# Loads of the sheared band issued by ScalarE, stores of T alone in SyncE's queue, four slots in DRAM

## The chip, the core and the metric

The kernel runs on one core of a Trainium2 chip. The metric is the device time of one execution in microseconds (us). The engines are named as in the profile: PE is TensorE (PEld its weight loads), DVE is VectorE, ACT is ScalarE, POOL is GpSimd, and SP is SyncE, which in this kernel does nothing but issue transfers. ACTq or SPq is an engine's instruction sequencer, which waits, branches and issues transfers while the engine's arithmetic may go on.

## What is computed

A layer norm feeds two branches, an attention with relative positions and a mixture of experts (top 2 of 8), and both are added to x. The change touches the attention alone, and there the term that adds q times the relative key:

```python
# x: (2, 2048, 256), 16 heads of 16, MAX_LEN 256; 2 batches x 16 heads = 32 heads below
rel_pos = jnp.arange(L)[None, :] - jnp.arange(L)[:, None] + (MAX_LEN - 1)
rel_k = relative_k[rel_pos]                       # out of range: wraps once, then clips
rel_v = relative_v[rel_pos]
scores = jnp.einsum('bhld,bhrd->bhlr', Q, K) * scale
scores = scores + jnp.einsum('bhld,lrd->bhlr', Q, rel_k)
attn = jax.nn.softmax(scores, axis=-1)
out = jnp.einsum('bhlr,bhrd->bhld', attn, V) + jnp.einsum('bhlr,lrd->bhld', attn, rel_v)
```

## The kernel before

The program has three stages: `project` (norm, q, k, v; up to about 180 us), `attend` (about 180 to 3440 us), and `mix` (output projection and experts). Only `attend` is changed.

`attend` works on 512 units. A unit is 128 query rows of one head, so a head has 16 units, and 2 heads (`STEP` = 32 units) make one turn of a loop in the program; `pipeline` writes the first 23 steps and the last ones out and loops over the rest. One step k does different parts of several units: the relative product T of unit k, the scores and their maximum of unit k-3, the row with the maximum of unit k-4 (`q_max`), the transposed scores and exponentials of unit k-5, the values of unit k-6, and the relative values of earlier half heads.

The path of T, with which the change deals, is this. PE multiplies the unit's queries by the relative keys (L875), 128 x 768. ACT copies the product from PSUM to `rel[k % 2]` (`rel_evac`, L1039, two copies of 128 x 384). SP stores it to `rel_scratch` in DRAM, a slot of 128 rows of 1280 words (L772, one or two transfers), and reads it back with a row pitch that is one word shorter (L762, `skew_src`), so that row p comes back shifted by p: the sheared band, up to 128 x 1152, in `skewed[u % 4]`. DVE adds the band to the scores when it looks for the maximum (`search_bank`, L1116 near the diagonal, L1120 elsewhere), and PE adds it in the transposed scores (L923).

Each engine runs its instructions in the order in which the program writes them. In step k, SP's are: wait until T of unit k-1 is stored (`s_gw`, L755) and until the band's buffer is free (`s_x`, L759), load the band of unit k-1 (L762), wait for ACT's copies of unit k (`s_ge`, L766) and for the load of unit k-2, which reads the same of the two slots (L769), store T of unit k (L772). In steps 5 to 10 of a head (`LOAD0` = 5) follow one q and one k transfer each for the next head (`load_stacks`, L703 and L706, both on one semaphore `s_stk`), in step 5 also the v rows (L712).

ACT's order in step k is: exponentials 0 and 1 of unit k-5 (L1047), the low half of the maximum (L1061), the two copies of T of unit k (L1039), exponentials 2 and 3, the copy of `q_max` of unit k-4 (L1071), and two or more casts of exponentials (L1055). The copy of T of unit k waits at L1037 until T of unit k-2 is stored, as there are two `rel` buffers. PE begins a step with the first two turned score tiles, which need `q_max`, and DVE searches the scores with the band. POOL makes the low parts of the exponentials (L839) and, in steps 7 to 10 of a head, the parts of the next head's v (L824 to L828).

Of the kernel before, what the change touches and what calls it, by code (L numbers as in the profile page):

```python
# [563 lines left out]
def attend(nc, hbm, keep):  # L564

    with ExitStack() as ctx:
# [36 lines left out]

        s_stk = [sem(f"b_stacks{i}") for i in range(2)]
        s_vi = [sem(f"b_v_in{i}") for i in range(2)]
# [89 lines left out]

        def load_stacks(sp, it, head, planes=range(6)):

            b = head % 2
            for j in planes:
                s, tile = j % 3, j // 3  # L700
                rows = bass.ds((it + head // 2) * DK, DK)
                r0 = tile * ROW_TILE + DK * s
                sp.dma_start(q_stack[b][r0:r0 + DK, :],  # L703
                             hbm["planes"][0, Q_PLANES[s], rows, b * L:(b + 1) * L]).then_inc(s_stk[b], 16)
                keys = hbm["planes"][1:1 + KINDS, K_PLANES[s], rows, b * L + tile * HALF_L:b * L + (tile + 1) * HALF_L]
                sp.dma_start(k_stack[b][r0:r0 + DK, :, :], keys.rearrange("v d n -> d v n")).then_inc(s_stk[b], 16)  # L706

# [5 lines left out]

        STK = 12 * 16

# [27 lines left out]
        def _(sp):  # L743
# [3 lines left out]
            sp.nop(nofuse=True)  # L747
            load_stacks(sp, 0, 0)
            load_v(sp, 0, 0)

            def step(it, k):
                u = k - 1
                if exists(it, u):

                    sp.wait_ge(s_gw[u % 2], stored(it, u))  # L755
                    sp.nop(nofuse=True)
                    if u >= 4:
                        for s in s_x:
                            sp.wait_ge(s, it * (2 * STEP) + 2 * (u - 3))  # L759
                            sp.nop(nofuse=True)  # L760
                    w = blocks(u % NB) * P
                    sp.dma_start(skewed[u % 4][:, 0:w], skew_src(u % 2, w)).then_inc(s_gr[u % 4], 16)  # L762
                u = k
                if exists(it, u):

                    sp.wait_ge(s_ge, it * (2 * STEP) + 2 * u + 2)  # L766
                    sp.nop(nofuse=True)
                    if u >= 2:
                        sp.wait_ge(s_gr[(u - 2) % 4], uses(it, u - 2, 4, 16))  # L769
                        sp.nop(nofuse=True)  # L770
                    for to, a, w in rel_pieces(u % NB):
                        sp.dma_start(hbm["rel_scratch"][u % 2, :, to:to + w], rel[u % 2][:, a:a + w]).then_inc(s_gw[u % 2], 16)  # L772
                if LOAD0 <= k % NB < LOAD0 + 6 and exists(it, (k // NB + 1) * NB):

                    head = k // NB + 1
                    if head >= 2 and k % NB == LOAD0:
                        for s in s_x:
                            sp.wait_ge(s, it * (2 * STEP) + 2 * NB * (head - 1))
                            sp.nop(nofuse=True)
                    load_stacks(sp, it, head, [k % NB - LOAD0])  # L780
                    if k % NB == LOAD0:
                        if head >= 2:
                            sp.wait_ge(s_vp, 2 + it * (2 * len(V_STAGES)) + (head - 1) * len(V_STAGES))
                            sp.nop(nofuse=True)
                        load_v(sp, it, head)
# [80 lines left out]
        def _(pe):  # L866
            def rel_products(it, k):

                c = k % NB
                if c == 0:  # L870

                    pe.wait_ge(s_stk[(k // NB) % 2], it * STK + (k // NB // 2 + 1) * STK)
                for tile in range(2):
                    wait_bank(it, "rel", k, tile)
                    nc.tensor.matmul(bank_of("rel", k, tile)[:, 0:RELN // 2],  # L875
                                     q_stack[(k // NB) % 2][tile_rows(tile), c * P:(c + 1) * P],
                                     keep["rk_stack"][tile_rows(tile), :], start=True, stop=True).then_inc(s_g, 1)

            def score_banks(it, k, pair):

                c, b = k % NB, (k // NB) % 2
                banks = (pair, pair + 2)
                lists = [[seg for seg in segments(c) if seg[0] == bank] for bank in banks]
                for bank in sorted(banks, key=lambda n: len(lists[banks.index(n)])):
# [146 lines left out]
        def _(act):  # L1031
# [17 lines left out]
            def high_part(it, u, e):  # L1049
# [6 lines left out]
                ins.then_inc(s_ha, 1)  # L1056

            def maximum_low(it, u):

# [15 lines left out]
            def step(it, k):  # L1075
# [9 lines left out]
                if turning:  # L1085
                    exponentials(it, k - LAG_X, 2)
                    exponentials(it, k - LAG_X, 3)
                if exists(it, k - LAG_A):
                    query_rows(it, k - LAG_A)
# [695 lines left out]
def program(nc, hbm):  # L1785
    with ExitStack() as ctx:
# [10 lines left out]
        hbm["planes"] = nc.dram_tensor("planes_scratch", (1 + KINDS, 2, D, TOK), FP16, kind="Internal").ap()  # L1797
        hbm["rel_scratch"] = nc.dram_tensor("rel_scratch", (2, P, RELW), FP32, kind="Internal").ap()
        hbm["v_rows"] = nc.dram_tensor("v_rows_scratch", (H, P, NT, DK), FP32, kind="Internal").ap()
# [58 lines left out]
```

## Time and profile before

| | |
|---|---|
| median of 3 runs | 3974.83 us (3958.41 to 4023.03) |
| the profiled execution | 4002.26 us, span 4000.5 us |
| busy share of the span | PE 87%, POOL 69%, ACT 66%, DVE 62% |
| `attend`, 200 to 3400 us | PE 2865, POOL 2561, ACT 2386, DVE 2096 of 3200 us |
| mean granted clock of PE | 0.913 (1.0 is 2.4 GHz, 0.5 is 1.2 GHz) |
| moved | 703 MB, of which queue q1 (all of SP's transfers) 674 MB |

A busy time is the union of an engine's instructions. Weight loads overlap matmuls, so PE's busy time counts stretches in which one is in flight, not work at full rate. Idle time stands with what ended it. A sequencer's waits aren't busy time; SP's are shown in a list of their own.

### The profile page before, as it was taken

The page shows a single profiled execution, that of the slowest core. Times are in us where ns is not written, and L with a number is a line of the kernel's source. Part 1 is how long each engine was busy: PE and PEld are TensorE (multiplying, and loading weights), DVE is VectorE, ACT ScalarE, POOL GpSimd, SP SyncE. Part 2 cuts the span into 40 slices and gives each one's busy share as a digit, 9 for nine tenths or more (in the row PEclk, how much of TensorE's full clock was granted, in tenths as well). Part 3 has the DMA queues.
Part 4 walks back from the last instruction along what each step waited for, and adds up shares of the span by engine and source line. Part 5 has one row for each costly group of instructions (what it writes and reads, how often), then busy time and mean ns, then how long its engine had stood idle before and what let it go on. Part 6 is the DMA issues. An engine that isn't in the chain of part 4 may idle for free. (4 is left out here: it accounts for less than half of the span.)

```text
span 4000.5 us, 177840 instructions
## 1 busy us (share of the span) xinstructions
PE 3468.4 (87%) x65430; PEld 2705.7 (68%) x65430; DVE 2470.0 (62%) x7245; ACT 2646.1 (66%) x5852; POOL 2748.4 (69%) x3015
## 2 busy tenths in 40 slices
PE   7488989898989898989898989899989899799991
PEld 4266767676767676666676767677767677559990
DVE  6366667666667666656675666666667666544443
ACT  3277777777767776767676777777778777224440
POOL 0187878787878787878787888787888788550006
PEclk9689999999989999989898999998999999659995
DMA  8765656565656565656565656565666565542224
GB/s 270 239 200 171 192 176 193 178 186 179 187 174 191 175 193 170 188 170 188 169 194 163 188 179 193 175 193 181 187 184 191 176 186 175 186 166 65 65 62 134
DMA packets 345830, 703.29 MB, mean 176 GB/s; under 512 B 58009, under 2 KB 157186, under 8 KB 343826
## 3 DMA queue, kind: packets, MB, share of 16 engines
q1 hardware_dynamic: 338706, 673.92, 54.5%
q0 software_dynamic: 6144, 16.79, 1.3%
q8 instruction: 556, 9.11, 0.9%
q14 instruction: 424, 3.47, 0.3%
HBM read 343.02 MB, written 347.46 MB: 173 GB/s over the span
## 5 line engine op out<-in xcount | busy, mean ns | idle before, releaser
L839 POOL TENSOR_TENSOR pt_near<-pt_full,pt_near 128x512 f16<-128x512 f32 (+3 forms) x2176 | 2000.8, 948 | 633.1 <-DVE pt_near L1140 565.6
L1047 ACT ACTIVATE pt_full<-pb,exp_bias 128x512 f32<-128x512 f32 x2048 | 1312.6, 693 | 582.0 <-PE pb L931 545.6
L1120 DVE TENSOR_REDUCE part_max<-pb 128x1 f32<-128x512 f32 (+3 forms) x1376 | 771.8, 575 | 513.0 <-DMA skewed<-rel_scratch 317.9
L1116 DVE CUSTOM_DVE_ANT_0 near_sum<-pb,skewed 128x512 bf16<-128x512 f32 (+3 forms) x1216 | 676.2, 572 | 339.3 <-PE pb L889 304.4
L983 PE MATMUL pb<-pt_near,table_high 128*128 128x64 f16 (+6 forms) x18432 | 873.7, 190 | 1.6 <-DVE rel_out L1163 0.8
L983 PE MATMUL pb<-pt_near,table_low 128*128 128x64 f16 (+6 forms) x9216 | 857.7, 191 | 0.0
L983 PEld LDWEIGHTS pb<-pt_near,table_high 128*128 128x128 f16 x18432 | 829.7, 99 | 1.9 <-DVE rel_out L1163 0.9
L983 PEld LDWEIGHTS pb<-pt_near,table_low 128*128 128x128 f16 x9216 | 800.3, 99 | 0.2 <-issue 0.2
L923 PE MATMUL pb<-ident,skewed 128*128 128x128 f32 x3840 | 674.8, 296 | 109.4 <-issue 54.2
L1039 ACT COPY rel<-pb 128x384 f32<-128x384 f32 x1024 | 439.4, 485 | 285.7 <-DMA rel_scratch<-rel 239.3
L957 PEld LDWEIGHTS pb<-v_head,pt_near 128*128 128x128 f16 x13440 | 435.3, 97 | 201.2 <-issue 138.7
L1140 DVE CAST pt_near<-pt_full 128x512 f16<-128x512 f32 (+3 forms) x1280 | 541.4, 473 | 5.4 <-ACT pt_full L1047 5.4
L923 PEld LDWEIGHTS pb<-ident,skewed 128*128 128x128 f32 x3840 | 433.6, 148 | 163.5 <-ACT pt_full L1047 80.8
L957 PE MATMUL pb<-v_head,pt_near 128*128 128x33 f16 x13440 | 518.1, 179 | 15.8 <-POOL pt_near L839 13.5
L889 PE MATMUL pb<-k_stack,q_stack 48*128 48x512 f16 (+3 forms) x2592 | 475.0, 348 | 52.6 <-DVE part_max L1116 28.8
L931 PE MATMUL pb<-q_max,k_stack 50*128 50x128 f16 x8192 | 422.2, 225 | 42.9 <-ACT pt_full L1047 37.2
L839 POOL TENSOR_TENSOR pt_far<-pt_full,pt_far 128x512 f16<-128x512 f32 (+3 forms) x416 | 440.1, 1058 | 0.0
L1055 ACT CAST pt_near<-pt_full 128x512 f16<-128x512 f32 (+3 forms) x896 | 432.6, 539 | 0.0
L931 PEld LDWEIGHTS pb<-q_max,k_stack 50*128 50x128 f16 x8192 | 239.6, 96 | 225.0 <-issue 125.3
L1439 POOL DMA_INDIRECT stage<-y_slots_scratch,slot x64 | 60.7, 949 | 366.0 <-DMA y_slots_scratch<-y_group 346.8
L1055 ACT CAST pt_far<-pt_full 128x512 f16<-128x512 f32 (+3 forms) x416 | 253.1, 608 | 0.0
L889 PEld LDWEIGHTS pb<-k_stack,q_stack 48*128 48x128 f16 x2592 | 149.1, 97 | 121.3 <-DVE part_max L1116 61.3
(182 smaller groups left out, 4046.4 us busy)
## 6 DMA issues: line engine op xcount, KB each, us to landing
skewed<-rel_scratch SPq DMA_DIRECT2D x256, 576.0 KB, 4.8
rel_scratch<-rel SPq DMA_DIRECT2D x416, 319.5 KB, 5.3
rel_scratch<-rel SPq DMA_DIRECT2D x320, 320.0 KB, 4.6
skewed<-rel_scratch SPq DMA_DIRECT2D x64, 512.0 KB, 4.5
skewed<-rel_scratch SPq DMA_DIRECT2D x64, 448.0 KB, 3.9
k_stack<-planes_scratch SPq DMA_DIRECT2D x192, 96.0 KB, 5.1
planes_scratch<-planes SPq DMA_DIRECT2D x64, 256.0 KB, 4.2
rel_scratch<-rel SPq DMA_DIRECT2D x64, 256.0 KB, 4.5
```

The source lines that it names most:

```text
L839: ins = nc.gpsimd.tensor_tensor(pt_piece(c, 1, a, z, near), pt_full[e][:, (a - 4 * g) * P:(z - 4 * g) * P], pt_piece(c, 0, a, z, near), AL ...
L889: ins = nc.tensor.matmul(ps[:, a - bank * CH:z - bank * CH], q_stack[b][tile_rows(tile), c * P:(c + 1) * P], k_stack[b][tile_rows(tile), k ...
L923: nc.tensor.matmul(x_ps[e % 2][:, (blk - 4 * g) * P:(blk - 4 * g + 1) * P], skewed[u % 4][:, col:col + P], keep["ident"][:, :], is_transpo ...
L931: ins = nc.tensor.matmul(x_ps[e % 2][:, i * P:(i + 1) * P], k_stack[b][tile_rows(tile, STACK + 2), kind_of(c, blk), col:col + P], q_max[u ...
L957: ins = nc.tensor.matmul(o_ps[:, i * VW:(i + 1) * VW], src[:, cols], rhs, start=(blk == 0 and part == 0), stop=(blk == NB - 1 and part == 1))
L983: ins = nc.tensor.matmul(acc[:, c0:c1, :], keep[table][:, w:w + P], pt_near[half][:, part, c0:c1, d - M_LO, a * SHIFTS:(a + 1) * SHIFTS], ...
L1039: nc.scalar.copy(rel[k % 2][:, n * half:(n + 1) * half], bank_of("rel", k, n)[:, 0:half]).then_inc(s_ge, 1)
L1047: nc.scalar.activation(pt_full[e][:, :], x_ps[e % 2][:, :], ACT.Exp, bias=exp_bias[:, 0:1]).then_inc(s_exp, 1)
L1055: ins = nc.scalar.copy(pt_piece(c, 0, a, z, near), pt_full[e][:, (a - 4 * g) * P:(z - 4 * g) * P])
L1116: ins = nc.vector.tensor_tensor_reduce(out=near_sum[:, col:col + z - a], in0=src, in1=skewed[k % 4][:, col:col + z - a], scale=1.0, scalar ...
L1120: ins = nc.vector.tensor_reduce(best, src, axis=AX.X, op=ALU.max)
L1140: ins = nc.vector.tensor_copy(pt_piece(c, 0, a, z, near), pt_full[e][:, (a - 4 * g) * P:(z - 4 * g) * P])
```

## The change

ACT now issues the band's load (`load_sheared`), once a step, behind exponentials 2 and 3 and ahead of the `q_max` copy. SP issues the stores of T, with no load between them. `rel_scratch` has four slots instead of two, so the store of unit k waits for the load of unit k-4. The next head's q and k transfers are issued one per step: q in steps 5 to 10 of a head, k in steps 10 to 15, on semaphores of their own; PE waits for the k ones where the first scores of a head are made. The transfers, their number and their sizes are the same.

```diff
-        s_stk = [sem(f"b_stacks{i}") for i in range(2)]
+        s_qin = [sem(f"b_queries{i}") for i in range(2)]
+        s_kin = [sem(f"b_keys{i}") for i in range(2)]
...
             def step(it, k):
-                u = k - 1
+                u = k
                 if exists(it, u):
 
-                    sp.wait_ge(s_gw[u % 2], stored(it, u))
+                    sp.wait_ge(s_ge, it * (2 * STEP) + 2 * u + 2)
                     sp.nop(nofuse=True)
                     if u >= 4:
-                        for s in s_x:
-                            sp.wait_ge(s, it * (2 * STEP) + 2 * (u - 3))
-                            sp.nop(nofuse=True)
-                    w = blocks(u % NB) * P
-                    sp.dma_start(skewed[u % 4][:, 0:w], skew_src(u % 2, w)).then_inc(s_gr[u % 4], 16)
-                u = k
-                if exists(it, u):
-
-                    sp.wait_ge(s_ge, it * (2 * STEP) + 2 * u + 2)
-                    sp.nop(nofuse=True)
-                    if u >= 2:
-                        sp.wait_ge(s_gr[(u - 2) % 4], uses(it, u - 2, 4, 16))
+                        sp.wait_ge(s_gr[u % 4], uses(it, u - 4, 4, 16))
                         sp.nop(nofuse=True)
                     for to, a, w in rel_pieces(u % NB):
-                        sp.dma_start(hbm["rel_scratch"][u % 2, :, to:to + w], rel[u % 2][:, a:a + w]).then_inc(s_gw[u % 2], 16)
-                if LOAD0 <= k % NB < LOAD0 + 6 and exists(it, (k // NB + 1) * NB):
-
-                    head = k // NB + 1
-                    if head >= 2 and k % NB == LOAD0:
+                        sp.dma_start(hbm["rel_scratch"][u % 4, :, to:to + w], rel[u % 2][:, a:a + w]).then_inc(s_gw[u % 2], 16)
+                if LOAD0 <= k % NB and exists(it, (k // NB + 1) * NB):
+
+                    head, j = k // NB + 1, k % NB - LOAD0
+                    if head >= 2 and j == 0:
...
-                    load_stacks(sp, it, head, [k % NB - LOAD0])
-                    if k % NB == LOAD0:
+                    if j < 6:
+                        load_queries(sp, it, head, [j])
+                    if j >= 5:
+                        load_keys(sp, it, head, [j - 5])
+                    if j == 0:
...
+                if c == 0 and pair == 0:
+
+                    pe.wait_ge(s_kin[b], it * STK + (k // NB // 2 + 1) * STK)
...
+            def load_sheared(it, u):
+
+                act.wait_ge(s_gw[u % 2], stored(it, u))
+                if u >= 4:
+
+                    for s in s_x:
+                        act.wait_ge(s, it * (2 * STEP) + 2 * (u - 3))
+                act.nop(nofuse=True)
+                w = blocks(u % NB) * P
+                act.dma_start(skewed[u % 4][:, 0:w], skew_src(u % 4, w)).then_inc(s_gr[u % 4], 16)
+
...
                 if turning:
                     exponentials(it, k - LAG_X, 2)
                     exponentials(it, k - LAG_X, 3)
+                if exists(it, k - 1):
+                    load_sheared(it, k - 1)
                 if exists(it, k - LAG_A):
                     query_rows(it, k - LAG_A)
...
-        hbm["rel_scratch"] = nc.dram_tensor("rel_scratch", (2, P, RELW), FP32, kind="Internal").ap()
+        hbm["rel_scratch"] = nc.dram_tensor("rel_scratch", (4, P, RELW), FP32, kind="Internal").ap()
```

SP's queue before, from the store of unit 13 of a head to the store of unit 15 (steps 13 to 15, ahead of the loop): a load of the band stands in front of each pair of stores, and its wait for `b_rel_stored` is the wait for the stores just above it.

```order
175 L772 DMA rel_scratch<-rel 128x640 [waits b_rel_on_chip,b_skewed3]
176 L772 DMA rel_scratch<-rel 128x639
177 L762 DMA skewed<-rel_scratch 128x1152 [waits b_rel_stored1,b_turned_scores0,b_turned_scores1]
178 L772 DMA rel_scratch<-rel 128x640 [waits b_rel_on_chip,b_skewed0]
179 L772 DMA rel_scratch<-rel 128x512
180 L762 DMA skewed<-rel_scratch 128x1024 [waits b_rel_stored0,b_turned_scores0,b_turned_scores1]
181 L772 DMA rel_scratch<-rel 128x640 [waits b_rel_on_chip,b_skewed1]
```

SP's queue after, steps 14 and 15 of a head (in the loop): stores wait for ACT's copies (`b_rel_on_chip`) and for a load four units back, and one transfer of the next head's k stands between.

```order
215 L765 REGISTER_ALU
216 L771 DMA rel_scratch<-rel 128x640 [waits b_rel_on_chip,b_skewed2]
217 L771 DMA rel_scratch<-rel 128x512
218 L715 DMA k_stack<-planes_scratch 16x3x1024
219 L765 REGISTER_ALU
220 L771 DMA rel_scratch<-rel 128x640 [waits b_rel_on_chip,b_skewed3]
```

SP no longer waits for a store to land. ACT's queue before, from the copies of T to the next step's first exponential:

```order
162 L1039 COPY rel<-pb 128x384 [waits b_rel_stored0,b_rel_product]
163 L1039 COPY rel<-pb 128x384 [waits b_rel_product]
164 L1047 ACTIVATE pt_full<-pb,exp_bias 128x512 [waits b_low,b_turned_scores0]
165 L1047 ACTIVATE pt_full<-pb,exp_bias 128x512 [waits b_low,b_turned_scores1]
166 L1071 CAST q_max<-pb 128x128 [waits b_turned_scores1,b_turned_scores0,b_max_turned]
167 L1055 CAST pt_near<-pt_full 128x512 [waits b_pt_used,b_exp]
```

And ACT's queue after, a step of the same kind:

```order
173 L1044 COPY rel<-pb 128x384 [waits b_rel_stored0,b_rel_product]
174 L1044 COPY rel<-pb 128x384 [waits b_rel_product]
175 L1052 ACTIVATE pt_full<-pb,exp_bias 128x512 [waits b_low,b_turned_scores0]
176 L1052 ACTIVATE pt_full<-pb,exp_bias 128x512 [waits b_low,b_turned_scores1]
177 L1072 DMA skewed<-rel_scratch 128x1152 [waits b_turned_scores1,b_rel_stored1,b_turned_scores0]
178 L1087 CAST q_max<-pb 128x128 [waits b_turned_scores1,b_turned_scores0,b_max_turned]
```

The load has come between the last exponential and the `q_max` copy, with the wait for the stores of the unit before (`b_rel_stored1` beside the copies' `b_rel_stored0`). Its waits for `b_turned_scores` are for the same tiles as the exponentials above it.

## Rows read from the trace of the kernel before

**Rows 1.** Windows: busy us per engine (instructions), PEclk, DMA share, GB/s; `attend`.

```profile
200.00:3400.00 3200.00, 2865.14 (x60899) 2237.03 (x60899) 2096.40 (x6454) 2385.52 (x5369) 2560.68 (x2825) 0.94 0.60 183
```

**Rows 2.** Waits, 200 to 3300 us: us in total, times, longest.

```profile
SPq L756 <- DMA rel_scratch<-rel: 1754.6, 475, 6.8
...
DVE part_max L1120 <- DMA skewed<-rel_scratch: 302.3, 157, 5.1
...
ACT rel L1039 <- DMA rel_scratch<-rel: 228.5, 170, 3.8
...
PE pb L923 <- issue: 54.2, 13, 5.9
```

**Rows 3.** SP's timeline in an even head: start us, duration us, issue.

```profile
2067.68 0.32 SPq L762 DMA_DIRECT2D skewed<-rel_scratch  x1
2068.22 0.80 SPq L772 DMA_DIRECT2D rel_scratch<-rel  x2
2074.15 0.32 SPq L762 DMA_DIRECT2D skewed<-rel_scratch  x1
```

**Rows 4.** SP's timeline in an odd head, and ACT's copy of T there.

```profile
2160.08 0.82 SPq L772 DMA_DIRECT2D rel_scratch<-rel  x2
...
2167.74 0.35 SPq L762 DMA_DIRECT2D skewed<-rel_scratch  x1
...
2167.50 0.86 ACT L1039 COPY rel<-pb 128x384 f32<-128x384 f32 x2 [3.00 <-DMA rel_scratch<-rel]
```

**Rows 5.** ACT's timeline in an even head; in brackets the idle time ahead.

```profile
2009.38 0.86 ACT L1039 COPY rel<-pb 128x384 f32<-128x384 f32 x2
...
2014.77 0.86 ACT L1039 COPY rel<-pb 128x384 f32<-128x384 f32 x2
...
2016.92 0.26 ACT L1071 CAST q_max<-pb 128x128 f16<-128x128 f32 x1
...
2018.81 1.27 ACT L1047 ACTIVATE pt_full<-pb,exp_bias 128x512 f32<-128x512 f32 x2 [0.59 <-PE pb L931]
...
2025.77 1.27 ACT L1047 ACTIVATE pt_full<-pb,exp_bias 128x512 f32<-128x512 f32 x2 [2.40 <-PE pb L931]
...
2030.95 1.27 ACT L1047 ACTIVATE pt_full<-pb,exp_bias 128x512 f32<-128x512 f32 x2 [0.61 <-PE pb L931]
```

**Rows 6.** PE's timeline: the picks of a half head; the start of a loop turn.

```profile
2022.91 1.94 PE L998 MATMUL pb<-pick_dim,rel_out 128*128 128x16 f32 x16
...
2128.37 1.11 PE L923 MATMUL pb<-ident,skewed 128*128 128x128 f32 x4 [4.52 <-issue]
```

**Rows 7.** One instruction per unit, L1071: first and last start.

```profile
L1071 ACT CAST q_max<-pb x512: 257/286/302, 194.4 to 3406.2; 128x128 f16<-128x128 f32 x171
```

**Rows 8.** Transfers: count, KB each, median us from issue to landing.

```profile
skewed<-rel_scratch SPq DMA_DIRECT2D x256, 576.0 KB, 4.8
rel_scratch<-rel SPq DMA_DIRECT2D x416, 319.5 KB, 5.3
...
y_slots_scratch<-y_group SPq DMA_DIRECT2D x39, 256.0 KB, 2.2
```

**Rows 9.** Landing times of the stores at L772; busy tenths of the DMA engines, 2060 to 2096.

```profile
DMA to landing us min/median/max: 2.0/4.7/8.0
...
DMA  4059998105879940489895109599800998910388
```

**Rows 10.** Windows, columns as in rows 1.

```profile
2036.00:2060.00 24.00, 21.78 (x470) 17.43 (x464) 19.04 (x50) 19.04 (x42) 23.43 (x28) 0.93 0.74 235
...
2120.00:2132.00 12.00, 6.93 (x139) 5.02 (x134) 4.75 (x15) 6.01 (x15) 4.55 (x4) 0.84 0.81 235
2132.00:2138.00 6.00, 5.89 (x113) 4.58 (x109) 3.27 (x11) 4.12 (x10) 5.39 (x7) 0.74 0.16 40
...
2156.00:2168.00 12.00, 8.24 (x164) 5.83 (x158) 7.04 (x27) 6.64 (x15) 7.54 (x11) 1.00 0.48 150
2168.00:2180.00 12.00, 10.46 (x199) 9.22 (x199) 5.04 (x17) 7.39 (x16) 7.29 (x10) 0.72 0.60 170
```

More of the change, by code:

```diff
@@ L694, in tile_rows, with load_queries @@
             return slice(tile * ROW_TILE, tile * ROW_TILE + n)
-        def load_stacks(sp, it, head, planes=range(6)):
+        def load_queries(sp, it, head, parts=range(6)):
             b = head % 2
-            for j in planes:
+            for j in parts:
                 s, tile = j % 3, j // 3
@@ L703, in load_stacks, with load_keys @@
                 sp.dma_start(q_stack[b][r0:r0 + DK, :],
-                             hbm["planes"][0, Q_PLANES[s], rows, b * L:(b + 1) * L]).then_inc(s_stk[b], 16)
+                             hbm["planes"][0, Q_PLANES[s], rows, b * L:(b + 1) * L]).then_inc(s_qin[b], 16)
+        def load_keys(sp, it, head, parts=range(6)):
+            b = head % 2
+            for j in parts:
+                s, tile = j % 3, j // 3
+                rows = bass.ds((it + head // 2) * DK, DK)
+                r0 = tile * ROW_TILE + DK * s
                 keys = hbm["planes"][1:1 + KINDS, K_PLANES[s], rows, b * L + tile * HALF_L:b * L + (tile + 1) * HALF_L]
-                sp.dma_start(k_stack[b][r0:r0 + DK, :, :], keys.rearrange("v d n -> d v n")).then_inc(s_stk[b], 16)
+                sp.dma_start(k_stack[b][r0:r0 + DK, :, :], keys.rearrange("v d n -> d v n")).then_inc(s_kin[b], 16)
         def load_v(sp, it, head):
@@ L712, in load_v @@
             sp.dma_start(v_in[b][:, :, :], src.rearrange("o p n d -> p (o n) d")).then_inc(s_vi[b], 16)
-        STK = 12 * 16
+        STK = 6 * 16
         def near_block(half, part, c, d, a, z):
@@ L747, in _ @@
             sp.nop(nofuse=True)
-            load_stacks(sp, 0, 0)
+            load_queries(sp, 0, 0)
+            load_keys(sp, 0, 0)
             load_v(sp, 0, 0)
             def step(it, k):
-                u = k - 1
-                if exists(it, u):
-                    sp.wait_ge(s_gw[u % 2], stored(it, u))
-                    sp.nop(nofuse=True)
-                    if u >= 4:
-                        for s in s_x:
-                            sp.wait_ge(s, it * (2 * STEP) + 2 * (u - 3))
-                            sp.nop(nofuse=True)
-                    w = blocks(u % NB) * P
-                    sp.dma_start(skewed[u % 4][:, 0:w], skew_src(u % 2, w)).then_inc(s_gr[u % 4], 16)
                 u = k
@@ L870, in rel_products @@
                 if c == 0:
-                    pe.wait_ge(s_stk[(k // NB) % 2], it * STK + (k // NB // 2 + 1) * STK)
+                    pe.wait_ge(s_qin[(k // NB) % 2], it * STK + (k // NB // 2 + 1) * STK)
                 for tile in range(2):
@@ L1056, in high_part @@
                 ins.then_inc(s_ha, 1)
+            def load_sheared(it, u):
+                act.wait_ge(s_gw[u % 2], stored(it, u))
+                if u >= 4:
+                    for s in s_x:
[3 more added lines that the diff above has]
+                act.dma_start(skewed[u % 4][:, 0:w], skew_src(u % 4, w)).then_inc(s_gr[u % 4], 16)
             def maximum_low(it, u):
```

## The prediction

> **What bounds the kernel now.** I read the windows first. In `attend`, which is 3,200 of 4,000 us, no engine is full: PE has something in flight 90% of the time, POOL 80%, ACT 75% [rows 1]. So some round of waits must set the pace, and the list of waits says which [rows 2]. SP waited 475 times, 1754.6 us in all, for the store of T to land before it could issue the load of the band. ACT waited 228.5 us in 170 steps for the same stores (its `rel` buffer is free only then), and DVE 302.3 us for the bands that are loaded behind them.
>
> SP's timeline shows the round. In an even head the band's load goes out at 2067.68, the stores of the next T 0.54 us later at 2068.22, and the next load at 2074.15, when those stores have landed [rows 3]. The store waits behind the load in SP's one queue, the next load waits for the store, and a turn takes 6.47 us. In an odd head the stores issued at 2160.08 are waited for until 2167.74, 7.66 us, so a turn takes 8.2 us; ACT sits idle 3.00 us before its copy of T at 2167.50, which is when they landed [rows 4]. Where the round doesn't bind, a step is shorter: ACT's copies of T follow each other at 2009.38 and 2014.77 (5.39 us), and first exponentials at 2025.77 and 2030.95 (5.18 us), and there ACT waits for PE, 0.59 and 0.61 us, not for a transfer [rows 5]. I take 5.3 us as a free step. The average over all units is (3406.2 - 194.4) / 511 = 6.285 us, 100.6 us a head [rows 7].
>
> **Is it the transfers' amount, or their waiting in turn?** Between 2060 and 2096 us the DMA engines' busy tenths run 4 0 5 9 9 9 8 1 0 and again: idle between one turn's landing and the next turn's first packets [rows 9]. That is a chain with gaps, not full engines. A wide unit moves 576 + 640 KB [rows 8], which at 5.3 us a step is 235 GB/s, and 235 GB/s was moved in 2036 to 2060 at a share of 0.74 [rows 10].
>
> **The change, part by part.**
>
> *SP's queue without the loads.* The stores of unit k no longer wait for the store of k-1 to land, nor lie behind a 576 KB load issued 0.54 us earlier. This unties the round above. The time that the store then takes has no row. Below, 256 KB alone land in 2.2 us [rows 8]; above, the longest landing at L772 is 8.0 us [rows 9]. The load still runs at the same time in part, now issued about 1.3 us after the store instead of before it. I take 5.3 us, the median that stands with a load in front [rows 8], as the side on which I would rather err.
>
> *ACT's new wait.* The store of T of unit k-1 must have landed when ACT comes to the load in step k. The time it has: from the end of the copies, 2009.38 + 0.86 = 2010.24, to the end of the next step's last exponential, at 2016.92 where `q_max` starts [rows 5]: 6.7 us. It needs up to 0.8 us for the two issues and 5.3 us to land, 6.1 us: no stall in an ordinary step, 0.6 us to spare. In odd heads it may stall at times. Queued behind the wait on ACT are the `q_max` copy and the casts; PE's turned scores and POOL's low parts wait for those.
>
> *ACT's issue.* On SP one issue lasts 0.32 us, and 0.54 us pass from it to the next [rows 3]. On ACT no row shows one, so the cost per unit lies between 0 (the sequencer issues while the exponentials still run) and 0.54 us. ACT waits 0.6 us a step for PE [rows 5], which covers even the upper end. I take 0. If the cover were gone, 512 x 0.54 = 276 us.
>
> *The band's landing.* DVE needs it about 1.3 steps after its issue or later (it is loaded in step k and searched in step k+2), some 7 us, and it takes 4.8 us [rows 8]. DVE's 302.3 us go, and cost nothing by themselves.
>
> *Four slots, and k a step later.* The wait for the load of unit k-4 is for one issued three steps before: 0. The k transfers end in step 15, and are first needed in step 3 of the next head, four steps later: 0. SP issues one of them behind a store instead of two, and with 0.8 us of stores [rows 3] in a step of 5.3 us it has time for either.
>
> **The sum.** A head after the change, from free steps: 14 steps of 5.3 us and 2 in which PE picks (1.94 us of matmuls at L998 [rows 6]; first exponentials 2018.81 and 2025.77, so 6.96 us [rows 5]) make 88.1 us. POOL is the next bound where it also makes the v parts: it was busy 23.43 of 24 us in 2036 to 2060 [rows 10]. I add 0.7 us in two steps, 1.4 us. What the change doesn't touch: at the start of a loop turn PE stands still, 4.52 us in the one shown [rows 6], 54.2 us in 13 [rows 2], and the clock is low afterwards (0.74 in 2132 to 2138 [rows 10]). About 6.8 us at 1.2 GHz instead of 2.4 lose at most 3.4 us. So (4.2 + 3.4) x 13 / 32 = 3.1 us a head. Together 92.6 us, against 100.6 us now: 8.0 us a head, 256 us in 32 heads.
>
> I check this against the waits. ACT's stalls are 228.5 us; 170 x 0.6 us of that would be spent waiting for PE anyway, which leaves 126 us. The other part is PE's clock. It is 0.94 in `attend` [rows 1], so 12% of 3200 us, 384 us, were at 1.2 GHz, with at most 192 us lost, of which 44 us belong to the loop turns: at most 148 us. They follow gaps in PE's work: in 2156 to 2168 PE was busy 8.24 of 12 us, and in 2168 to 2180 the clock was 0.72; the same after 6.93 of 12 us in 2120 to 2132 [rows 10]. 126 + 148 = 274 us, close to 256.
>
> That is what is gained if every stall and every fall of the clock outside the loop turns goes. Some will stay: late stores in odd heads, POOL's two steps, the picks. I take four fifths, 205 us: 4002 - 205 = 3797 us for the profiled execution. The median shown is 0.9931 of it (3974.83 / 4002.26), so 3771 us; I say 3770.
>
> The Trainium skill's page "DMA: Bandwidth & Descriptors" (section "Issuing engines are not separate DMA queues") says that transfers started by different engines run on the same 16 DMA engines and interleave, and that spreading them only saves the time of issuing. By that rule alone the change would save little. It speaks of bandwidth, and the gaps in the DMA row are at odds with it as a bound here; the first rival below is its case. The page's section on queues adds that each DMA engine takes turns between SP's and ACT's rings; no run before shows it.
>
> **The rivals.**
>
> *Only the issue is saved (chance 0.13).* The load and the store still share the engines and stretch each other, so that a turn is shorter by no more than the 0.54 us from load to store. 170 stalled steps x 0.54 = 92 us, and about half of it is lost again where ACT issues (170 x 0.32 = 54 us). Then 4002 - 38 = 3964, median 3937. For: in 2036 to 2060 the DMA share is already 0.74 [rows 10]. Against: the idle tenths [rows 9].
>
> *ACT pays for the issue in full (0.04).* 4002 + 276 - 205 = 4073, or with the 0.6 us of cover near 3800. The middle, 3936, is a median of 3909. Against it stands ACT's idle time.
>
> *ACT is held at the load: slower (0.06).* The wait stands in an engine that the whole round runs through. From the load's place to the end of the copies of the next step but one ACT needs 2014.77 + 0.86 - 2016.92 + 5.39 = 4.1 us [rows 5]. If a store lands L us after its copies, two steps take L + 4.1 us. That is as slow as the 6.47 us of now from L = 8.8 us on. With the longest landing, 8.0 us [rows 9], and both issues, and some more for the load that runs with it, L = 9.6 and a step is 6.85 us. In the 11 wide units of each head 352 x 0.4 = 140 us are lost: 4142, median 4114. It needs stores that land twice as late as their median, all the time.
>
> *Nothing moves (0.03).* PE or POOL bound it at the present pace, the stalls being covered. The free steps of 5.2 to 5.4 us speak against it.
>
> **The numbers.** The forecast has 0.74, with 3710 to 3860 as its own range. About 2% can be told from no change in this kernel, that is 3895. Faster: the forecast, and the luckier part of the second rival, 0.77. Within 2%: 0.17. Slower: 0.06. Below, all 256 us give 3746 or a median of 3720, and free steps 0.1 us shorter another 45 us less; I set 3690. Above I reach to 3895, which leaves out most of the rivals.
>
> **What would show it.** SP's waits for its own stores are gone and ACT waits at the new load by less than 0.3 us on average. ACT no longer waits for `rel_scratch<-rel` ahead of its copies, and DVE's waits for `skewed` fall under 50 us. `q_max` copies stand 5.9 us apart on average instead of 6.285. PEclk in `attend` rises from 0.94 to 0.96 or more. The loop turns' stalls stay near 54 us. `project` and `mix` keep their times. The forecast is wrong if stores land 7 us or more after issue although no load lies in front, if ACT's waits at the load add up to over 150 us, or if the steps are free of transfer waits and yet take over 6 us.

## Result and profile after

The changed kernel takes 3818.0 us, median of 4 runs (3809.99 to 3820.11), beside 3977.4 us for the kernel before. The ratio is 0.9611 (95% interval 0.9572 to 0.9649): 3.9% faster. The forecast of 3770 was 48 us too low; the range of 3690 to 3895 holds the time. The profiled executions went from 4002.26 to 3820.08 us, 182 us, where 205 were forecast and 256 worked out as the most.

The page of the changed kernel, its span and engines, and the queues (packets, MB, share of 16 engines). q10 is new: it carries ACT's loads.

```profile
span 3818.3 us, 177264 instructions
...
PE 3355.8 (88%) x65430; PEld 2639.2 (69%) x65430; DVE 2542.1 (67%) x7245; ACT 2650.5 (69%) x5852; POOL 2750.4 (72%) x3015
...
q1 hardware_dynamic: 264978, 422.23, 32.4%
q10 hardware_dynamic: 73728, 251.69, 25.1%
```

The changed kernel's windows view of `attend`, columns as in [rows 1]. `attend` is shorter, so this window stops at 3220 us, just ahead of the last `q_max` copy, as the one of before does.

```profile
200.00:3220.00 3020.00, 2749.69 (x60814) 2169.71 (x60813) 2163.31 (x6437) 2384.35 (x5357) 2556.82 (x2819) 0.97 0.64 193
```

Its `q_max` copies, first and last start (the line that answers to [rows 7]):

```profile
L1087 ACT CAST q_max<-pb x512: 262/265/302, 188.6 to 3227.5; 128x128 f16<-128x128 f32 x171
```

They stand (3227.5 - 188.6) / 511 = 5.947 us apart, where it was 6.285 [rows 7]. From the first copy to the last it is 3038.9 us instead of 3211.8, so 172.9 us came from the spacing. The first copy is 5.8 us earlier, and the end behind the last one is 3.5 us shorter. That is the whole 182 us; `project` and `mix` hardly moved. The granted clock rose from 0.94 to 0.97.

The changed kernel's waits, 200 to 3300 us (us in total, times, longest), against [rows 2]:

```profile
ACT q_max L1087 <- DMA rel_scratch<-rel: 76.4, 62, 2.6
...
PE pb L928 <- issue: 72.2, 14, 6.3
...
PE pb L962 <- POOL pt_far L841: 47.0, 88, 0.9
...
PE pb L928 <- ACT q_max L1087: 22.2, 41, 1.4
```

SP's waits for its stores (1754.6 us), ACT's ahead of its copies (228.5) and DVE's for the band (302.3) [rows 2] have no row any more. In their place ACT waits 62 times, 76.4 us in all, for a store at the new load; it shows as idle time of the `q_max` copy behind it. The waits under "issue" at L928, nearly all of them the stall at the start of a loop turn, have grown from 54.2 to 72.2 us.

Landing times in the changed kernel (count, KB each, median us), against [rows 8]. The row of 319.5 KB is the second transfer of a store (in 12 of its 13 cases a head), the row of 320.0 KB the first of a wide one:

```profile
skewed<-rel_scratch ACTq DMA_DIRECT2D x256, 576.0 KB, 5.1
rel_scratch<-rel SPq DMA_DIRECT2D x416, 319.5 KB, 4.8
rel_scratch<-rel SPq DMA_DIRECT2D x320, 320.0 KB, 2.9
```

The store is only 0.5 us faster than with a load in front of it (5.3 us [rows 8]). The next two views say why. First an ordinary step, ACT's timeline of the changed kernel (start, duration, engine, what; ACTq is the issue of a DMA on ACT):

```profile
2057.02 0.85 ACT L1044 COPY rel<-pb 128x384 f32<-128x384 f32 x2
2057.74 0.72 ACT L1052 ACTIVATE pt_full<-pb,exp_bias 128x512 f32<-128x512 f32 x1
2057.80 0.33 ACTq L1072 DMA_DIRECT2D skewed<-rel_scratch  x1
2058.33 0.71 ACT L1052 ACTIVATE pt_full<-pb,exp_bias 128x512 f32<-128x512 f32 x1
2058.90 0.30 ACT L1087 CAST q_max<-pb 128x128 f16<-128x128 f32 x1
```

And SP's timeline of the changed kernel there:

```profile
2058.01 0.86 SPq L771 DMA_DIRECT2D rel_scratch<-rel  x2
```

In the program the load stands behind both exponentials. It was issued at 2057.80, before the second of them began and 0.21 us **ahead** of the store, which has to wait for the end of the copies. So an ACT issue runs beside ACT's arithmetic (good for its cost), and the load lost the distance of 1.3 us to the store that the forecast had given it.

Second, a late store: ACT's timeline of the changed kernel, the load issued in step 14 of an odd head and then step 15 (in brackets the idle time ahead and its releaser).

```profile
1295.65 0.33 ACTq L1072 DMA_DIRECT2D skewed<-rel_scratch  x1
...
1299.98 0.85 ACT L1044 COPY rel<-pb 128x384 f32<-128x384 f32 x2
1300.70 1.29 ACT L1052 ACTIVATE pt_full<-pb,exp_bias 128x512 f32<-128x512 f32 x2
1304.06 0.33 ACTq L1072 DMA_DIRECT2D skewed<-rel_scratch  x1
1304.57 0.27 ACT L1087 CAST q_max<-pb 128x128 f16<-128x128 f32 x1 [2.58 <-DMA rel_scratch<-rel]
```

The store it waits for, on SP's timeline of the changed kernel, with the transfer of the next head's k behind it:

```profile
1296.00 0.79 SPq L771 DMA_DIRECT2D rel_scratch<-rel  x2
1296.89 0.55 SPq L715 DMA_DIRECT2D k_stack<-planes_scratch  x1
```

and in the list of transfers of 1296 to 1304 us:

```profile
rel_scratch<-rel SPq DMA_DIRECT2D x1, 256.0 KB, 7.6
```

The load of step 14 had gone out at 1295.65, 0.35 us ahead of this store. The store's second piece landed after 7.6 us, and PE's transposes at L928 waited behind ACT:

```profile
1304.89 0.66 PE L928 MATMUL pb<-ident,skewed 128*128 128x128 f32 x4 [1.13 <-ACT q_max L1087]
```

ACT lost 2.58 us and PE only 1.13, since PE's matmuls of the relative values (L988) filled the rest.

### The profile page after: what moved, and what is told of

Read it like the earlier page. It is cut to its first block and busy times, and to the rows that moved or that the text cites. A ratio compares the mean times of both kernels' runs of the same rounds, so it can differ in the third digit from the quotient of the medians.

```text
span 3818.3 us, 177264 instructions
## 1 busy us (share of the span) xinstructions
PE 3355.8 (88%) x65430; PEld 2639.2 (69%) x65430; DVE 2542.1 (67%) x7245; ACT 2650.5 (69%) x5852; POOL 2750.4 (72%) x3015
## 5 line engine op out<-in xcount | busy, mean ns | idle before, releaser
L988 PE MATMUL pb<-pt_near,table_high 128*128 128x64 f16 (+6 forms) x18432 | 845.2, 188 | 12.4 <-issue 11.2
L988 PE MATMUL pb<-pt_near,table_low 128*128 128x64 f16 (+6 forms) x9216 | 828.7, 188 | 7.1 <-issue 6.8
L988 PEld LDWEIGHTS pb<-pt_near,table_high 128*128 128x128 f16 x18432 | 798.5, 98 | 16.4 <-issue 15.3
L928 PE MATMUL pb<-ident,skewed 128*128 128x128 f32 x3840 | 659.4, 291 | 145.5 <-issue 72.2
L988 PEld LDWEIGHTS pb<-pt_near,table_low 128*128 128x128 f16 x9216 | 777.7, 97 | 6.9 <-issue 6.5
L1158 DVE CAST pt_near<-pt_full 128x512 f16<-128x512 f32 (+3 forms) x1280 | 618.3, 532 | 5.4 <-ACT pt_full L1052 5.4
L928 PEld LDWEIGHTS pb<-ident,skewed 128*128 128x128 f32 x3840 | 421.5, 145 | 202.5 <-ACT pt_full L1052 80.2
L841 POOL TENSOR_TENSOR pt_far<-pt_full,pt_far 128x512 f16<-128x512 f32 (+3 forms) x416 | 449.0, 1079 | 0.0
L894 PE MATMUL pb<-k_stack,q_stack 48*128 48x512 f16 (+3 forms) x2592 | 433.3, 343 | 5.7 <-DMA k_stack<-planes_scratch 2.1
L877 PE MATMUL pb<-rk_stack,q_stack 48*128 48x384 f16 x1024 | 173.3, 332 | 38.6 <-DMA q_stack<-planes_scratch 37.8
## 6 DMA issues: line engine op xcount, KB each, us to landing
rel_scratch<-rel SPq DMA_DIRECT2D x416, 319.5 KB, 4.8
```

What stands on the lines that cost most here:

```text
L841: ins = nc.gpsimd.tensor_tensor(pt_piece(c, 1, a, z, near), pt_full[e][:, (a - 4 * g) * P:(z - 4 * g) * P], pt_piece(c, 0, a, z, near), AL ...
L894: ins = nc.tensor.matmul(ps[:, a - bank * CH:z - bank * CH], q_stack[b][tile_rows(tile), c * P:(c + 1) * P], k_stack[b][tile_rows(tile), k ...
L928: nc.tensor.matmul(x_ps[e % 2][:, (blk - 4 * g) * P:(blk - 4 * g + 1) * P], skewed[u % 4][:, col:col + P], keep["ident"][:, :], is_transpo ...
L988: ins = nc.tensor.matmul(acc[:, c0:c1, :], keep[table][:, w:w + P], pt_near[half][:, part, c0:c1, d - M_LO, a * SHIFTS:(a + 1) * SHIFTS], ...
L1158: ins = nc.vector.tensor_copy(pt_piece(c, 0, a, z, near), pt_full[e][:, (a - 4 * g) * P:(z - 4 * g) * P])
```

## The experiments

My theory after the result: the round of waits on SP is gone as forecast, and what is missing from the 256 us lies in the distance from the store's issue to the load's. The rivals: it is the issue on ACT that costs; or slots and spread transfers carry part of the gain; or code or POOL's work sets what is left. Diffs are against the changed kernel where nothing else is said.

**The same order, all on SP (e1).** SP issues the store of unit k and behind it the load of unit k-1.

```diff
                         sp.dma_start(hbm["rel_scratch"][u % 4, ...]).then_inc(s_gw[u % 2], 16)
+                u = k - 1
+                if exists(it, u):
+                    sp.wait_ge(s_gw[u % 2], stored(it, u))
...
+                    sp.dma_start(skewed[u % 4][:, 0:w], skew_src(u % 4, w)).then_inc(s_gr[u % 4], 16)
...
-                if exists(it, k - 1):
-                    load_sheared(it, k - 1)
```

> The changed kernel with one part undone: SP issues the band's load again, but behind the store of the next unit instead of ahead of it (four slots and the spread q and k transfers stay). Untying theory (the gain came because no store waits for the load's turn and the store before): within 1% of the changed kernel's 3818 us, that is 3790 to 3860, SP's longest waits are for ACT's copies, ACT waits for stores under 80 us in all. Separate-queue theory (the gain needs the load in ACT's own ring): the load lies behind 640 KB of stores in one ring, DVE waits for the band by some 300 us again, and the time is 3930 us or more.

Measured: 3751.0 us, ratio 0.9425 (0.9383 to 0.9466), 67 us below the changed kernel and below the range that either theory gave. The list of waits of this kernel no longer has ACT waiting for a store, and PE's other waits are small:

```profile
PE pb L939 <- issue: 60.0, 13, 5.9
...
PE pb L973 <- POOL pt_far L852: 43.5, 80, 0.9
```

Its landing times, and SP's timeline of a step:

```profile
skewed<-rel_scratch SPq DMA_DIRECT2D x256, 576.0 KB, 5.3
rel_scratch<-rel SPq DMA_DIRECT2D x416, 319.5 KB, 3.1
```

```profile
2059.78 0.80 SPq L771 DMA_DIRECT2D rel_scratch<-rel  x2
2060.88 0.32 SPq L782 DMA_DIRECT2D skewed<-rel_scratch  x1
```

With the load 1.10 us behind, the store's second piece lands in 3.1 us, not 4.8. So ACT's queue isn't needed for the gain. How much the order gives by itself shows beside e3 below, which has the same four slots, the same spread transfers and SP alone, but the load ahead of the store: 3894.9 against 3751.0 us, 144 us for the order. The new order with two slots and paired transfers was not run.

**The load on ACT alone (e2).** The kernel before with only the load moved to ACT: two slots, and q and k issued together as before.

```diff
--- kernel before
-                    sp.dma_start(skewed[u % 4][:, 0:w], skew_src(u % 2, w)).then_inc(s_gr[u % 4], 16)
...
+                if exists(it, k - 1):
+                    load_sheared(it, k - 1)
```

> The kernel before with one part of the change alone: ACT issues the band's load; two slots, and q and k transfers in pairs in steps 5 to 10. Untying theory: most of the gain is here, but the store of unit k now waits for the load of k-2, which ACT issued 5.4 - 1.3 = 4.1 us before the copies of unit k end and which takes 4.8 to 5.1 us: stores go out about 1 us late and ACT waits at the load by 100 to 200 us in all: 3840 to 3900 us. Slots-and-spreading theory (four slots and one transfer per step make the gain): 3940 us or more.

Measured: 3821.9 us, ratio 0.9605 (0.9561 to 0.965), as the changed kernel, and below the 3840 to 3900 expected. The moved load carries the whole gain. The waits of this kernel:

```profile
ACT q_max L1071 <- DMA rel_scratch<-rel: 117.5, 91, 2.8
...
SPq L759 <- DMA skewed<-rel_scratch: 128.7, 124, 3.3
```

ACT's wait at the load is longer than the 76.4 us of the changed kernel, and with two slots SP waits for a load two units back in 124 steps, 128.7 us in all, before it can store. Yet the time is the same within the intervals, so the slots and the spread are worth nothing that can be measured once the load is on ACT at this place.

**Slots and spread, with the load ahead of the store on SP.** Both together (e3), then each alone on the kernel before (e8 the slots, e9 the spread).

```diff
--- kernel before, both
-                    sp.dma_start(skewed[u % 4][:, 0:w], skew_src(u % 2, w))...
+                    sp.dma_start(skewed[u % 4][:, 0:w], skew_src(u % 4, w))...
...
-                    load_stacks(sp, it, head, [k % NB - LOAD0])
+                    if j < 6:
+                        load_queries(sp, it, head, [j])
+                    if j >= 5:
+                        load_keys(sp, it, head, [j - 5])
```

> The other parts alone: four slots and q and k one per step, but SP issues the load ahead of the store as before. Untying theory: the round of 6.5 to 8 us is intact, SP waits over 1500 us for its stores, and the time is 3940 to 3990 us. Slots-and-spreading theory: 3860 us or less.

> The kernel before with four slots in DRAM alone. e3 (four slots and spread transfers, SP's order as before) gained 83 us where I had put 0. Slots theory: half or more of it is here, 3930 us or less. Spreading theory: the wait for the load of k-2 was always over when SP came to it (it waits first for the store of k-1, issued behind that load), so 3978 us within 0.5%.

> The kernel before with the next head's q and k transfers one per step alone (two slots). Spreading theory: nearly all of e3's 83 us, 3885 to 3920 us, with ACT's waits for stores in steps 10 to 15 of a head down and those in steps 0 and 1 as before. Slots theory: 3978 us within 0.5%.

Measured: both 3894.9 us, ratio 0.9788 (0.9743 to 0.9833), between what the two theories gave; slots alone 3913.6, 0.9830 (0.9769 to 0.9891); spread alone 3914.9, 0.9873 (0.9810 to 0.9935). All three intervals lie below 1, but none of the gains is clear of 2%. SP's round of waits is still there in the run with both (200 to 3300 us as in [rows 2]; us in total, times, longest):

```profile
SPq L766 <- DMA rel_scratch<-rel: 1761.4, 499, 6.4
...
ACT rel L1055 <- DMA rel_scratch<-rel: 132.2, 113, 3.7
```

Its turns are shorter: the 576 KB load lands in 4.5 us (4.8 before [rows 8]) and the store's second piece in 5.0 (5.3 before), and ACT's waits fall from 228.5 to 132.2 us. Each part shows most of this by itself (151.6 us of ACT waits with the slots, 143.0 with the spread), so they don't add up. Why either makes a transfer 0.2 to 0.3 us faster stays open; no wait on a slot is in the trace of before.

**The load later on ACT.** Behind the last casts (e5), or behind the `q_max` copy (e6).

```diff
--- e5
-                if exists(it, k - 1):
-                    load_sheared(it, k - 1)
                 if exists(it, k - LAG_A):
                     query_rows(it, k - LAG_A)
...
                     high_part(it, k - LAG_X, 3)
+                if exists(it, k - 1):
+                    load_sheared(it, k - 1)
```

> The changed kernel with ACT's load moved from ahead of the q_max copy to the end of ACT's step, behind the casts (about 1.3 us later). If ACT's stalls at the load (76 us in 62 steps, the q_max copy behind them) cost time: they fall under 20 us, PE no longer waits for q_max, and the time is 3775 to 3800 us. If they are covered by ACT's waits for PE: 3818 us within 0.4%. If the band now comes too late for DVE, its waits for skewed appear (over 50 us) and the time is 3840 us or more.

> The changed kernel with the load one instruction later, behind the q_max copy and ahead of the casts (0.15 to 0.3 us later; e5 has it 1.3 us later still, at the end of the step). If what the stall costs is the q_max copy that waits behind it: 3766 to 3785 us, near e5. If it is the nearness of the load to the store, which then share the DMA engines (e5's stores land in 3.1 us, the changed kernel's in 4.8): the landing stays near 4.5 us, ACT still waits 40 us or more, now ahead of the casts, and the time is 3795 to 3820 us.

Measured: e5 3765.7 us, ratio 0.9471 (0.9433 to 0.9510), 9 us below its best case; e6 3773.5 us, 0.9508 (0.9458 to 0.9557). They beat the changed kernel by 52 and 44 us. Of e5, the list of waits has this behind ACT, and this landing time:

```profile
PE pb L928 <- ACT q_max L1087: 3.0, 7, 0.7
```

```profile
rel_scratch<-rel SPq DMA_DIRECT2D x416, 319.5 KB, 3.1
```

In e6 what is left of ACT's wait stands behind the `q_max` copy, ahead of the casts:

```profile
ACT pt_near L1060 <- DMA rel_scratch<-rel: 17.4, 17, 1.5
```

I took the distance between the two issues for every unit from the timelines: the load's start, less the start of the copies of T plus 0.99 us (the median from the copies' start to the store's issue). For the kernel before, where SP issues the store right behind the load, it is taken from SP's own two issues. Beside it stands the landing time of the row of 319.5 KB.

| kernel | load behind store, median (lowest tenth) | store lands in | ACT waits for a store | time |
|---|---|---|---|---|
| before | -0.55 (-0.62) | 5.3 | 228.5 | 3977 |
| changed | 0.28 (-0.34) | 4.8 | 76.4 | 3818 |
| e6 | 0.58 (0.17) | 4.2 | 17.4 | 3774 |
| e1 | 1.09 (0.74) | 3.1 | none | 3751 |
| e5 | 1.29 (1.21) | 3.1 | none | 3766 |

In the changed kernel 22% of the loads go out ahead of their step's store (26% against the store's own issue in the trace). The distance orders the landing times, and these order ACT's waits. It does so inside the changed kernel too. Among its 256 widest stores (both pieces of 320 KB) the second piece lands in 5.8 us where the load is some 0.25 us ahead (median of 47), in 5.6 where it is 0.5 us behind (23), in 4.4 at 0.75 us (35) and in 3.6 at 1.0 us (43). Whether the load is in the same queue as the store (e1) or in another (e5) makes no difference to the store, 3.1 us both times.

What the stall costs is less clear. e6 was meant to part two readings: that the time goes with the `q_max` copy held behind the wait (3766 to 3785 us expected), or with the nearness of load and store (3795 to 3820, with 40 us of waits or more). Its time came out as in the first, with PE's waits for `q_max` down from 22.2 to 3.1 us, while its store landed in 4.2 us, close to the 4.5 of the second. One instruction's move changed both the distance and what stands behind the wait, so the 44 us can't be put down to either alone.

The Trainium skill's page "DMA: Bandwidth & Descriptors" (section "Queues, rings and completion order") says that each DMA engine takes turns between the rings, packet by packet. The trace fits it in kind: in the changed kernel a load in a ring of its own, issued 0.28 us behind, still stretched the store to 4.8 us. In these runs a ring of its own gave the store no priority.

**What an issue on ACT costs (e7).** e5 with each load in two transfers of 64 rows, so one more issue in each of 512 units.

```diff
--- e5
-                act.dma_start(skewed[u % 4][:, 0:w], skew_src(u % 4, w)).then_inc(s_gr[u % 4], 16)
+                for r0 in (0, P // 2):
...
+                    act.dma_start(skewed[u % 4][r0:r0 + P // 2, 0:w], src).then_inc(s_gr[u % 4], 16)
```

> e5 (load at the end of ACT's step, 3766 us) with the load as two transfers of 64 rows each: one more issue on ACT per unit, 512 in all, the same bytes. If an issue holds ACT's arithmetic for its 0.33 us and ACT is on the path: up to 169 us more, 3850 to 3935 us. If ACT's waits for PE cover it: 3766 us within 0.5%, with ACT's idle time ahead of L1047 down by some 100 us. A gain would mean that two smaller transfers land earlier.

Measured: 3791.3 us, ratio 0.9547 (0.9496 to 0.9597), 26 us above e5 and a little more than the 0.5% allowed for full cover: some 0.05 us a unit (the intervals overlap a little). The issues of this kernel at their line (shortest, median, longest in ns; first and last start):

```profile
L1075 ACTq DMA_DIRECT2D skewed<-rel_scratch x1024: 452/556/2153, 182.0 to 3180.0; - x171
```

An issue of 0.56 us costs a tenth of that: ACT's arithmetic covers it. The rival in which ACT pays in full is out.

**The loop turn (e10).** e1 with ten more steps peeled off ahead of the loop, so that a turn begins in another step of the head.

```diff
--- e1
-PEEL = LAG_O + 1
+PEEL = LAG_O + 11
```

> e1 (3751 us) with the turn of the program's loop ten steps later, at step 1 of a head instead of step 7 (PEEL 33 for 23), where the load moves 384 KB or less and no q or k transfer is under way. If PE's stall at the loop's start (60 us in 13 turns in e1, 72 in the changed kernel, 54 before) is code that arrives behind 1.1 MB of data: 2.5 to 3.5 us a stall instead of 4.6, 15 to 30 us less in all, 3715 to 3740 us. If it is the fetch itself: the stalls keep 4.5 us each and the time stays within 0.5% of 3751 us.

Measured: 3792.1 us, ratio 0.9550 (0.9505 to 0.9595), 41 us worse than e1, which neither case had foreseen. PE's waits in this kernel:

```profile
PE pb L939 <- issue: 90.0, 26, 5.2
```

Now there are two stalls a turn (13 turns, 26 stalls) instead of one, the first of 4.1 to 5.2 us and the second of 2.0 to 2.7. During the second the DMA engines are busy for 2 to 8% of the time. So the idea that PE's code arrives late because data transfers are in its way doesn't explain this one, and the first has hardly shrunk from e1's 3.4 to 5.9 us although less data moves beside it. What it is instead no run shows. Why the turn's stall grew from 54 us to 72 (68 in e5, 60 in e1) stays open.

**POOL's v parts.** e1 with the eight v parts of the next head one to a step (steps 7 to 14) instead of two to a step (7 to 10) (e11); then this with the later loop turn (e12); then e1 with the parts kept out of steps 10 to 13 (e13).

```diff
--- e1, e11
-                if V0 <= k % NB < V0 + len(V_STAGES) // 2 and exists(it, (k // NB + 1) * NB):
-
-                    for j in range(2):
-                        v_part(it, k // NB + 1, 2 * (k % NB - V0) + j)
+                if V0 <= k % NB < V0 + len(V_STAGES) and exists(it, (k // NB + 1) * NB):
+
+                    v_part(it, k // NB + 1, k % NB - V0)
--- e1, e13
+        V_STEPS = {7: (0, 1), 8: (2, 3), 9: (4,), 14: (5, 6), 15: (7,)}
```

> e1 with POOL's eight parts of the next head's v one per step in steps 7 to 14 instead of two per step in steps 7 to 10. If POOL is the bound in steps 10 to 12 (6.02, 6.45, 5.75 us in e1, PE waits for pt_far and pt_near there, 43 us for pt_far alone): those steps fall to 5.5 us on average, PE's waits for POOL by more than half, and the time by 30 to 50 us: 3700 to 3720 us. If POOL's load only moves on: within 0.5% of 3751 us.

> Both edits on e1. If they act at different places, their gains add: 3675 to 3705 us, the fastest of all. If one wait takes the place of the other, it is no better than the better of the two.

> e1 with POOL's eight v parts where POOL has room: two in steps 7 and 8, one in 9, two in 14, one in 15, none in 10 to 13. e11 (one per step in 7 to 14, 3706 us) made step 13, in which the low parts alone take 6.5 us of POOL, 7.59 us instead of 6.97. If POOL's own time per step decides: step 13 back at 7.0 us, steps 10 to 12 as in e11, 14 and 15 unchanged at 5.0 and 5.2: 20 us less than e11, 3680 to 3695 us. If steps 7 and 8 with two parts push POOL behind again as in e1: 3706 us or more.

Measured: e11 3706.1 us, ratio 0.9343 (0.9300 to 0.9386), the fastest of all and in its range; e12 3743.8, 0.9434 (0.9391 to 0.9478), so the later turn costs 38 us here as it cost 41 on e1; e13 3734.4, 0.9388 (0.9329 to 0.9448), faster than e1 but outside both of its cases. PE's waits for POOL (`pt_far` and `pt_near`) fall from 63.8 us in e1 to 19.9 in e11. e11's windows view of `attend`, POOL's being the fifth busy time:

```profile
200.00:3200.00 3000.00, 2797.18 (x61710) 2206.38 (x61709) 2267.56 (x6554) 2388.86 (x5404) 2635.30 (x2871) 0.97 0.62 200
```

The mean time of a step by its place in the head (us, from the first exponentials of one step to those of the next, over all 511 steps between them):

```
step     0    1    2    3    4    5    6    7    8    9   10   11   12   13   14   15
before 6.34 6.31 5.49 5.37 5.38 6.90 7.34 5.84 5.12 5.45 6.38 6.92 6.49 9.22 5.53 6.44
after  5.38 5.38 5.49 5.37 5.38 6.90 7.83 6.27 5.16 5.79 6.07 6.30 5.70 7.03 5.06 6.03
e1     5.31 5.38 5.49 5.37 5.38 6.90 7.57 5.80 5.09 5.34 6.05 6.42 5.76 6.92 4.96 5.16
e11    5.32 5.38 5.49 5.37 5.38 6.90 7.32 5.90 5.12 5.26 5.32 5.41 5.54 7.53 4.98 5.17
```

With the parts spread, steps 10 to 12 fall from 18.2 to 16.3 us, and step 13 rises by 0.6. e13 was to keep the first and undo the second. Step 13 did come back to 7.0 and step 11 stayed at 5.4, but step 10 was 6.08 and steps 0 and 1 rose to 5.69 and 5.86. My reading, which no run tests by itself, is that POOL's backlog was carried into other steps, and that an even load on POOL is worth more than an idle POOL in the step of the picks.

## Why the prediction was right, and where not

**The bound, the sign, the forecast case: shown.** Undone alone (e3), SP's round and ACT's waits come back; done alone (e2), the whole gain is there. The transfer waits of SP, ACT's copies and DVE are gone. The clock is 0.97 where 0.96 or more was forecast, and the spacing 5.947 where 5.9 was given. Of the check by waits, the clock's part can be read from the trace: between the first and the last `q_max` copy PE stood at 1.2 GHz for 381 us before and for 194 us after. That is 187 us less, worth 94 us at most (an estimate: half of it), where all but the loop turns had been put at 148.

**The size of a free head: right, in part because errors cancel.** The sum had 92.6 us for a head without transfer waits. e1, which has none, takes 92.9 (its row above, summed), so the floor of 256 us below before was near: 3746 for the profiled execution, beside 3758 of e1's. Inside the sum POOL's steps 10 to 12 take 2.3 us more than free ones (18.2 against 15.9), not 1.4. Against that, the nine free steps (0 to 4, 8, 9, 14, 15) take 5.28 us and not 5.3, the two of the picks 13.8 and not 13.9, and steps 6 and 7, where the loop turns fall, are 2.8 us above free ones, not 3.1. The 6.8 us at 1.2 GHz per turn stand in no row; the two windows shown at the turn give 7.0 (12 us at 0.84 and 6 us at 0.74). In the changed kernel the turns were not "untouched": PE's stalls there are 72.2 us in all, and steps 6 and 7 are 3.5 us above free ones.

**ACT's new wait: the term that was mis-sized.** The text had "issued about 1.3 us after the store instead of before it". I took ACT's place in program order, behind the exponentials, for a place in time. The load went out 0.28 us behind the store (median), in 22% of the steps ahead of it. So the store took 4.8 us, near the 5.3 that I had kept on the safe side. From the end of the copies to the landing of the whole store it is 5.2 us in the median, but in about one unit of eight more than the 6.7 us that ACT gives it; there ACT stands. The price is the difference to the kernels without the late stores: 52 us (e5) to 67 us (e1), though e6 leaves open how much of it is the distance and how much the `q_max` copy behind the wait. By step (the table above), 1.79 of the 2.24 us a head between changed kernel and e1 are in steps 15, 9 and 7. The 76.4 us of ACT's waits at the load are of the same size.

**The share kept back: too small.** One fifth of 256 us, 51 us, was set aside for late stores, POOL and picks. The profiles left 256 - 182 = 74 us: 62 that divide the changed kernel from e1 (3820 - 3758), and 12 that divide e1 from the floor. This is the 23 us between forecast and profiled result. The other 25 of the 48 us come from the scaling: I had multiplied by 0.9931, the median of before over its profiled execution, but the changed kernel's profiled execution stands at its median (3818.0 / 3820.08 = 0.9995).

**ACT's issue at 0: right within 0.05 us a unit** (e7), and for the reason given, that the issue runs beside the exponentials. It is the same fact that spoiled the term above; I used it for the cost and not for the time.

**DVE's waits cost nothing by themselves: not tested alone.** They are gone in e1, e5 and the changed kernel alike.

**Slots and k a step later, 0: right in this change (e2), wrong on the old order**, where they give 1.3 to 2.1% (e3, e8, e9). That they add nothing here is luck in part: no reason was given that would have told the two cases apart.

**The rivals.** "Only the issue is saved" gave 38 us; 182 came. It was refuted for a reason that I had: the time of the DMA engines was not the bound. "ACT is held at the load" named the mechanism that did appear, but with stores at 4.8 us, not 9.6, it holds ACT in 62 steps and not in all. The Trainium skill's page "DMA: Bandwidth & Descriptors" (section "Issuing engines are not separate DMA queues") is borne out in its own field: all the transfers still share the same engines, and a load issued by ACT stretched SP's store to 4.8 us. What changed the time was the order, as e1 shows with no second issuing engine at all.

## What to carry to other kernels

When a store and a load that depends on an earlier store alternate in one queue, put the store that is waited for first, and the large load behind it (here 1.1 to 1.3 us served); which engine issues them mattered less. A DMA issue on ACT was nearly free here, but it went out as soon as its semaphores allowed and not when the arithmetic above it in the program was done: place it by the time at which its waits fall, and look at what stands behind it. And once the first bound is gone, look at what the next engine does unevenly; here spreading POOL's helper work was worth 45 us more (e11).

## What was unexpected about the hardware

- ACT issued a DMA at 2057.80, while two exponentials that stand above it in the program ran until about 2059.0.
- The same store transfer of 319.5 KB lands in 5.3, 4.8, 4.2 and 3.1 us as the load that shares the engines is issued -0.55, 0.28, 0.58 and 1.09 us behind it.
- Four slots in DRAM instead of two gave 1.7% (e8) though no slot was waited for.
- Starting the loop turn in another step of the head turned one stall of PE into two (60.0 to 90.0 us in 13 turns), the second with the DMA engines all but idle.
- Whether SP issues the band's load ahead of the next store or behind it, with nothing else changed, is 144 us of 3895 (e3 and e1).
